# Cross-attention's output step run batch by batch between the units of grouped attention

## What is computed

```
x = x + fp8_product(layernorm(x), ctx)                    # 1
x = x + ternary_ffn(layernorm(x))                         # 2
x = x + cross_attention(layernorm(x), ctx)                # 3: 16 heads of 16, int8 rounding of input and of output
n = layernorm(x);  h = n / rms(n) * ln_w                  # 4: 32 query heads, 8 key heads of 64
n = n + grouped_causal_attention(rope(h @ wq), rope(h @ wk), h @ wv) @ wo
x = x + n + top4_of_16_experts(n / rms(n) * ff_ln_w)
```

## Time and profile before

| | |
|---|---|
| three runs | 795.86, 798.83, 798.04 us; median 798.04 |
| the profiled execution | 799.3 us, its span 797.5 us (1.8 us lie around the span) |
| busy in the span | PE 602.7 us, DVE 557.8, POOL 461.7, ACT 432.0 |
| chain that ended last | PE 50%, DVE 26%, POOL 8%, issue 6%, ACT 6%, DMA 2% |
| cross-attention | about 163 to 285 us |
| the middle | 285 to 319 us |
| prologue | 319 to 341 us |
| the loop | 341 to 613 us |
| router, experts, output | 613 to 797 us |

### The profile page before, as it was taken

The page is one execution under the profiler, slowest core; times in us unless marked ns, Lnnn a source line. Parts: engine busy times, 40 slices in busy tenths (PEclk is TensorE's granted clock), DMA queues, the critical chain, the costliest instruction groups (busy, mean ns, idle before and its releaser), DMA issues.

```text
span 797.5 us, 16092 instructions
## 1 busy us (share of the span) xinstructions
PE 602.7 (76%) x5533; PEld 430.8 (54%) x5533; DVE 557.8 (70%) x1420; ACT 432.0 (54%) x1213; POOL 461.7 (58%) x424
## 2 busy tenths in 40 slices
PE   0226989168888834789999999999885269999960
PEld 0113666156566623457777776777764236666640
DVE  5999558877978877866677577577555755555545
ACT  4823533168768821366666665766652227766640
POOL 1051554258977932278798698677533246777750
PEclk9998897679999977999999999999999559999995
DMA  9500130127545530033032522312501812333427
GB/s 300 187 1 1 37 122 2 57 75 229 161 134 191 159 120 1 0 67 67 15 93 55 92 43 41 68 27 55 185 2 57 356 49 90 108 105 110 104 84 261
DMA packets 83465, 77.97 MB, mean 98 GB/s; under 512 B 49408, under 2 KB 75776, under 8 KB 82880
## 3 DMA queue, kind: packets, MB, share of 16 engines
q1 hardware_dynamic: 78880, 64.33, 27.7%
q0 software_dynamic: 4512, 12.71, 5.5%
HBM read 47.46 MB, written 18.55 MB: 83 GB/s over the span
## 4 chain that ended last, share of the span: by engine, by line
PE 50%; DVE 26%; POOL 8%; issue 6%; ACT 6%; DMA 2%; SPq 1%; POOLq 0%; ACTq 0%; DVEq 0%
PE ps L1787 9%; PE ps L2076 8%; PE ps L2002 5%; PE ps L1986 5%; PE ps L1969 5%; PE ps L2099 4%; PE ps L1844 2%; ACT arena L973 2%; PE ps L1714 2%; DVE arena L1493 2%; POOL arena L831 2%; DVE tiny L1486 2%; PE ps L1732 1%; ACT arena L1058 1%; PE ps L2051 1%
## 5 line engine op out<-in xcount | busy, mean ns | idle before, releaser
L1058 ACT ACTIVATE arena<-ps,tiny 128x128 f32<-128x128 f32 (+1 forms) x256 | 103.9, 418 | 53.8 <-DVE tiny L1486 53.8
L831 POOL TENSOR_TENSOR arena<-arena,tiny 128x512 f32<-128x512 f32 x64 | 93.9, 1467 | 62.9 <-DVE tiny L1497 62.7
L1493 DVE COPY arena<-ps 128x512 f32<-128x512 f32 x64 | 44.3, 692 | 75.3 <-PE ps L1969 75.3
L2076 PE MATMUL ps<-arena 128*128 (+1 forms) x282 | 70.6, 387 | 1.2 <-issue 0.7
L1787 PE MATMUL ps<-arena,xt_hi 128*128 128x512 f16 (+1 forms) x224 | 63.1, 367 | 3.6 <-DVE xt_lo L1275 3.0
L866 POOL DMA_INDIRECT arena<-h_store,arena x47 | 46.0, 979 | 33.3 <-DVE arena L1616 19.3
L1986 PE MATMUL ps<-arena 128*64 128x128 f32 x768 | 56.1, 280 | 11.3 <-DVE arena L1501 11.3
L1486 DVE TENSOR_REDUCE tiny<-ps 128x4 f32<-128x512 f32 x64 | 60.9, 952 | 1.2 <-PE ps L1954 0.9
L1630 DVE SCALAR_TENSOR_TENSOR ps<-ps,arena 128x256 f32<-128x256 f32 x47 | 20.3, 433 | 56.3 <-ACT arena L1110 56.3
L1986 PEld LDWEIGHTS ps<-arena 128*64 128x64 f32 x768 | 41.4, 136 | 32.3 <-issue 23.2
L1952 PE MATMUL ps<-arena 128*128 128x128 f16 (+1 forms) x256 | 58.5, 247 | 0.2 <-ACT arena L1037 0.2
(11 more groups left out here) (293 smaller groups left out, 1724.7 us busy)
## 6 DMA issues: line engine op xcount, KB each, us to landing
e_store<-arena SPq DMA_DIRECT2D x13, 768.0 KB, 4.2
arena<-e_store SPq DMA_DIRECT2D x13, 768.0 KB, 8.6
work<-w_dram SPq DMA_DIRECT2D x27, 256.0 KB, 4.6
xn<-w_dram SPq DMA_DIRECT2D x21, 256.0 KB, 4.7
arena<-w_gate_up_t_dram SPq DMA_DIRECT2D x2, 1024.0 KB, 9.0
arena<-wq_dram SPq DMA_DIRECT2D x2, 1024.0 KB, 7.5
arena<-wo_dram SPq DMA_DIRECT2D x2, 1024.0 KB, 5.2
work<-y_store SPq DMA_DIRECT2D x8, 256.0 KB, 5.2
```

The costliest lines, as they stand in the source:

```text
L831: nc.gpsimd.tensor_tensor(p, p, arec[:, u % 4, :].unsqueeze(2).broadcast_to([P, GH, L]), ALU.mult)\
L1058: nc.scalar.activation(ap_[u % 3][:, h, 0:L], head_scores(u, h), ACT.Exp, bias=anm[:, u % 4, h:h + 1], accum_out=asum[:, u % 4, h:h + 1]). ...
L1493: nc.vector.tensor_copy(apt[:, u % 2, 0, :], ps[:, 3, :]).then_inc(a_pt, 1)
L2076: last = mm(ps[:, 2 + i % 2, :], xg[:, i % 2, x_half * KB + k, :], weights(hidden_weights(slot, w_half, k), i), start=(n == 0), stop=(n == 5))
```

## The change

The end of step 3, from the rounding to the second turn, is now a set of steps for one batch (two tiles). Batch 0 takes them during the last batches of cross-attention and straight after it; batches 1 to 3 take them between the units of the loop, one batch ahead: the batch `nb` that follows the batch of the pass. In each batch of passes, counted 0 to 15: DVE rounds at 14 and 15 of the batch before (batch 1: just ahead of the loop), PE turns at 2, PE multiplies by `wo` at 6, DVE adds and takes statistics at 6, POOL makes the roots at 7, DVE makes `xn` and `work` at 8, PE turns at 9. The sides are placed anew: query group 2 of each batch moves into its own batch, six sides of batch 0 instead of eight run ahead of the loop, and the next batch's keys and values come at 10 to 15. The raw expert buffers change places, `work2` first and `xn` second, the expert after the 13 stored ones goes into `work2`, and the wait for the stored cuts moves from DVE to ACT's first pass.

```
-    own = [(3, 0), (3, 1), (4, 0), (4, 1)]
-    following = [(KEY, 0), (KEY, 1), (VAL, 0), (VAL, 1), (1, 0), (1, 1), (2, 0), (2, 1)]
-    at = [0, 1, 2, 4, 5, 6, 8, 9, 10, 12, 13, 14]
+    own = {0: (2, 0), 1: (2, 1), 4: (3, 0), 5: (3, 1), 7: (4, 0), 8: (4, 1)}
+    following = {10: (KEY, 0), 11: (1, 0), 12: (KEY, 1), 13: (1, 1), 14: (VAL, 0), 15: (VAL, 1)}
...
+TURN_O, OUT_O, TURN_H = 2, 6, 9
...
+            later += [(n, h, u + 2) for h in range(2 if c == KEY else 1)]
...
-        e_raw = [t[:, 0:EW // D, :].rearrange("p t d -> p (t d)") for t in (xn, work2)]
+        e_raw = [t[:, 0:EW // D, :].rearrange("p t d -> p (t d)") for t in (work2, xn)]
...
+        def mid_bank(b, first):
+            return 7 if b else first
```

POOL:

```
+            def root_mid(b):
+                ts = batch_tiles(b)
+                pool.wait_ge(stats_ready, 3 + b + 1)
+                link(nc.gpsimd.tensor_scalar(shifted[:, ts], meanvar[:, ts, 1], LN_EPS, 0.0, ALU.add, ALU.add))
+                link(nc.gpsimd.tensor_tensor(rstd[:, ts], shifted[:, ts], half_neg[:, ts], ALU.pow))
+                link(nc.gpsimd.tensor_tensor(shifted[:, ts], rstd[:, ts], rstd[:, ts], ALU.mult))
+                link(nc.gpsimd.tensor_tensor(shifted[:, ts], shifted[:, ts], meanvar[:, ts, 1], ALU.mult))
+                link(nc.gpsimd.tensor_scalar(shifted[:, ts], shifted[:, ts], LN_EPS, 0.0, ALU.add, ALU.add))
+                nc.gpsimd.tensor_tensor(rstd2[:, ts], shifted[:, ts], half_neg[:, ts], ALU.pow).then_inc(rstd_ready, 1)
...
+                    if n == STORED - 1:
+                        root_mid(0)
                     cut_lo(n)
-            root_layernorm(3)
...
+                if i % AU == OUT_O + 1 and i // AU + 1 < B:
+                    root_mid(i // AU + 1)
```

ACT (`turned_o_hi` and `turned_h_hi` write `xt_hi` of one batch after its turn):

```
+                if i % AU == TURN_O + 1 and i // AU + 1 < B:
+                    turned_o_hi(i // AU + 1)
+                if i % AU == TURN_H + 1 and i // AU + 1 < B:
+                    turned_h_hi(i // AU + 1)
+                if i == 0:
+                    for k in range(2):
+                        act.wait_ge(e_kept[k], 16 * len(range(k, STORED, 2)))
```

DVE (`turned_o_lo` and `turned_h_lo` write `xt_lo`; `o_scale` is the row maximum, one scaling and one reciprocal):

```
+            def o_quantise(b):
+                tiles = range(b * TB, (b + 1) * TB)
+                for t in tiles:
+                    last = nc.vector.tensor_scalar(work[:, t, :], work[:, t, :], recip[:, t:t + 1], 127.0, ALU.mult, ALU.min)
+                link(last)
...
+            def add_cross(b):
+                vec.wait_ge(xo_out, (b + 1) * TB)
+                for t in range(TB):
+                    row = b * TB + t
+                    nc.vector.scalar_tensor_tensor(x[:, row, :], ps[:, mid_bank(b, 1), t * D:(t + 1) * D], 1.0 / WS,
+                                                   x[:, row, :], ALU.mult, ALU.add).then_inc(xo_added, 1)
...
+            def normal_rows(b):
+                vec.wait_ge(rstd_ready, 3 + b + 1)
+                tiles = range(b * TB, (b + 1) * TB)
+                for t in tiles:
+                    last = nc.vector.tensor_scalar(xn[:, t, :], x[:, t, :], meanvar[:, t, 0:1], rstd[:, t:t + 1],
+                                                   ALU.subtract, ALU.mult)
+                link(last)
+                for t in tiles:
+                    last = nc.vector.tensor_scalar(work[:, t, :], xn[:, t, :], rstd2[:, t:t + 1], None, ALU.mult)
+                last.then_inc(src_ready, 1)
...
+                    if more and b == B - 2 and i == XU:
+                        vec.wait_ge(x_normed, TB + 1)
+                        o_scale(0)
+                        o_quantise(0)
...
+                    if not more and i == XU:
+                        turned_o_lo(0)
...
+                else:
+                    add_cross(0)
...
+            vec.wait_ge(e_cut_ready, STORED - 1)
+            normal_rows(0)
+            turned_h_lo(0)
...
+            o_scale(1)
+            o_quantise(1)
             for i in range(UNITS + 3):
...
+                if i % AU == TURN_O + 1 and i // AU + 1 < B:
+                    turned_o_lo(i // AU + 1)
+                if i % AU == TURN_H + 1 and i // AU + 1 < B:
+                    turned_h_lo(i // AU + 1)
                 for n in sides_at(i):
                     if n in ROPES:
                         rope(n)
+                if i // AU + 1 < B:
+                    if i % AU == OUT_O:
+                        add_cross(i // AU + 1)
+                    elif i % AU == TURN_H - 1:
+                        normal_rows(i // AU + 1)
+                if i // AU + 2 < B:
+                    if i % AU == AU - 2:
+                        o_scale(i // AU + 2)
+                    elif i % AU == AU - 1:
+                        o_quantise(i // AU + 2)
```

PE (`turn_mid` turns four blocks of 128 by 128; `project_o` is the product by `wo`, twelve matmuls of 256 columns):

```
+                    if not more and i == XU:
+                        pe.wait_ge(x_masked, B * XU)
+                        turn_mid(0, 0, 0)
+                    if not more and i == XU + 2:
+                        project_o(0)
...
             def project(n):
...
+                if u >= 0:
+                    side_bank_free(u)
+                    if u % AU > TURN_H and b:
+                        pe.wait_ge(xt_ready, 8 + 2 * b + 2)
...
                 for n in sides_at(i):
                     project(n)
+                if i // AU + 1 < B:
+                    nb, at = i // AU + 1, i % AU
+                    if at in (TURN_O, OUT_O, TURN_H):
+                        side_bank_free(i)
+                    if at == TURN_O:
+                        turn_mid(nb, 0, 7)
+                    elif at == OUT_O:
+                        project_o(nb)
+                    elif at == TURN_H:
+                        turn_mid(nb, 1, 7)
                 if 2 <= i < UNITS + 2:
                     a_values(i - 2)
```

More of the change, by code:

```diff
@@ L98, in turns_in_order @@
              (2, 0, -1, 4, "act"), (3, 0, -1, 3, "vec")]
-    at = {(3, 0): 2, (3, 1): 3, (4, 0): 5, (4, 1): 7, (1, 0): 13, (1, 1): 14, (2, 0): 15, (2, 1): 17}
-    keys = {(0, 0): 8, (0, 1): 9, (1, 0): 10, (1, 1): 11}
     later = []
[L102 to L109, removed]
+    for n, (b, c, t, u) in enumerate(SIDE):
+        if n >= 4 and c != VAL:
+            later += [(n, h, u + 2) for h in range(2 if c == KEY else 1)]
     return order + [(n, h, u, None, "dma") for n, h, u in later]
@@ L1397, in cross_attend, with turned_h_lo @@
+            def turned_h_lo(b):
+                vec.wait_ge(xt_hi_ready, 8 + 2 * b + 2)
+                for k in range(KB):
+                    last = nc.vector.scalar_tensor_tensor(xt_lo[:, k, batch_tokens(b)],
+                                                          ps[:, mid_bank(b, 3), k * S:(k + 1) * S], ln_w[:, k:k + 1],
+                                                          xt_hi[:, k, batch_tokens(b)], ALU.mult, ALU.subtract)
+                last.then_inc(xt_ready, 1)
             def cross_attend(b, more):
@@ L1883, in cross_attend, with turn_mid, project_o @@
                     last.then_inc(x_turned_back, 1)
+            def turn_mid(b, step, bank):
+                pe.wait_ge(src_ready, 2 + 2 * b + step + 1)
+                for k in range(KB):
+                    for t in range(TB):
+                        at = k * S + t * P
+                        last = nc.tensor.transpose(ps[:, bank, at:at + P], work[:, b * TB + t, k * P:(k + 1) * P],
+                                                   ident[:, :])
+                last.then_inc(blocks_transposed, 1)
+            def project_o(b):
+                pe.wait_ge(xt_ready, 8 + 2 * b + 1)
+                for t in range(TB):
+                    rows = slice((b * TB + t) * P, (b * TB + t + 1) * P)
+                    products(ps[:, mid_bank(b, 1), t * D:(t + 1) * D],
+                             [((xt_hi[:, k, rows], xt_lo[:, k, rows]), (xwo_hi[:, k, :], xwo_lo[:, k, :]))
+                              for k in range(KB)]).then_inc(xo_out, 1)
             project_q(0)
```

146 lines of the change are left out of this document (82 added, 64 removed).

## The result

The changed kernel takes 805.89 us (median of 4 runs, 804.64 to 809.06), the kernel before 797.87 beside it: ratio 1.0106, 95% interval 1.0081 to 1.013. It is slower by 1.1%; the forecast was 794. Its profiled execution has a span of 803.8 us against 797.5.

A forecast was written before the change was run, and what follows sets the result against it. Middle and prologue were taken as bound by chained waits, the loop by its chain from ring maximum to copy, and by PE with two sides. 799.3 - 24.5 + 20 = 794.8, less 1.3: 793.5, rounded up to 794; range 783 to 807.

The forecast's parts named there:

- Steps 1 and 2: Middle: batch 0's rounding on DVE shows 0.9 us; its turn, split and product end cross-attention 1.3 later, at 287.1.
- Step 3: Middle: POOL's roots for batch 0 start about 285.7, take 4.8 us and end at 290.6.
- Step 4: Middle: batch 0's rows take 1.5 us, turn and split 3.0; first side at 295.1 instead of 319.26.
- Step 5: Prologue, first side to first maximum: 21.1 us, with two ropes fewer, batch 1's rounding and 1.3 for a slow first side.
- two ropes fewer, 4.4: Prologue: leaving out two ropes ahead of the loop saves 4.4 us.
- Slots: Loop: PE's added turns and product in the unit pairs cost 0.9 us a batch (0 to 2.2).
- Key side at 10: Loop pass 10: PE is blocked waiting for DVE's split `turned_h_lo`, 1.65 us a batch (0.8 to 2.4).
- Roots at 7, rows at 8: Loop pair 8-9: POOL's roots delay normalising, DVE's rows wait for POOL; 3.0 us a batch (0.5 to 6).
- slower rival: Loop passes 8 and 15: DVE's row steps queue behind POOL, 5 us a batch more, so 809; chance 18%.
- The rival that gaps take the most of it: Loop: idle gaps absorb most added work, leaving 2.6 us a batch; 781 to 788 us; chance 25%.
- Late keys: Loop: next batch's keys turned too late, its first units wait 4 us, three times: 806; chance 7%.
- Wrong if batches cost over 77 us: Loop: the forecast's sign of being wrong, batches of passes under 70 us or over 77.

The follow-up runs named there:

- late cut: Changed kernel with POOL's last stored cut step (low halves of expert 12) behind DVE's four row steps of batch 0: 800.21 us, ratio 1.0057.
- sides-alone kernel: Kernel before with only the new order of sides and ropes, nothing of the middle moved: 808.26 us, ratio 1.0143.
- sides alone with fitted cut steps: Kernel before with the new order of sides and cut steps at passes 3, 4, 20, 32, 35, 36, 48, 51, 52: 804.69 us, ratio 1.0102.
- combined kernel: Changed kernel with fitted cut steps, key side behind the values, batch 1's rounding early and the last stored cut step late: 790.08 us, ratio 0.9906.
- doubled roots: Changed kernel with POOL's six linked root steps made twice at passes 7, 23 and 39: 810.18 us, ratio 1.0162.
- side 8 moved: Kernel with all four edits, but query sides at 0, 1, 3, 4, 5, 7 and cut steps at other passes: 800.89 us, ratio 1.0026.

## Why the prediction was wrong

**The gain, 20.2 instead of 24.5.** Steps 1 and 2 and the start of the roots held (285.75 against 285.7). Step 3 was 2.1 too dear: the roots of two columns took 2.7 us, `pow` 0.71 each. Step 4 was 3.6 too cheap: from roots to first side 8.1 instead of 4.5, because the rows stood beside `cut_lo(12)`, whose store I had looked at but not what it does to DVE beside it; the late cut shows it. Step 5 was 2.9 too cheap, 24.0 instead of 21.1: "two ropes fewer, 4.4" failed (1.1 in the sides-alone kernel; behind the fourth rope the chain runs over ACT's copies), while the rounding, 3.5 us, showed in full.

**The loop, 27.6 instead of 20: the step that failed is "Slots", 0.9 per batch.** I priced it by PE's pairs, 3.6 in all with batch 3. The sides alone measure 14.4: about half for slots (1.9 in batch 2, 2.1 in batch 3, where cut steps make no difference) and half for cut steps that keep their passes while POOL's rope sums move into them. I went through the change by its new operations; the steps that stay at fixed passes were not among them. The earlier trace rows show POOL without a gap around a side; whether POOL has one behind pass 12 or 24 in the new order was never asked. The sum of the step is also off by itself: four pairs of 8.12 in 67.31 leave 8.7 for the others and not 8.6, and six of these with 8.3 and 7.9 make 68.4, so 1.1 by its own rule; that is small beside the rest.

**Key side at 10.** Issuing it later gave 5.7 back, against 5.0 forecast for the whole step. The wait was 2.4, 1.7 and 2.2, at the upper end, and one clock drop of 1.6 came with it. This is not all of its price: in the combined kernel, without that wait, the three passages are still 4.4 longer in all than in the sides alone with fitted cut steps. In the loop of before PE never stands more than 1.0 us for another engine.

**Roots at 7, rows at 8, the rest.** 27.6 - 14.4 - 5.7 leaves 7.5 for all else, where I had 11.4. Pair 8-9 came to 10.5, 13.5 and 10.8, near the 10.9 and the 12.8 behind a long cut step; that it fits is partly luck. The roots ahead of the rope sum were to make the normalising 2.5 late; at 2.7 us instead of 4.8 it came just in time, and only doubled roots show that chain. What fills the pair is DVE's rows, which wait for whole POOL instructions (the two `xn` steps take 1.49, 4.27 and 2.46 us instead of 0.73; all four rows are 1.4, 4.4 and 1.7 longer than alone). That was the slower rival's mechanism. Its place and sign were right for pass 8; it does not carry the result, since without those rows the kernel is still 0.6% slower than before, and the rounding at 14 and 15, which it charged too, cost nothing. The rival that gaps take the most of it falls: batches cost 6.3 to 11.6 more. Late keys did not show. "Wrong if batches cost over 77 us" came true in batch 1.

The Trainium skill, GPSIMD Engine Reference, Specifications, names contention for VectorE instructions in a two-port mode or with two SBUF inputs. The row steps have one wide SBUF input, and no run shows in which mode they ran; this case shows them waiting for POOL to the end of its instruction, 4.31 us against 0.73.

Open: what sets the price of the slots. With fitted cut steps passages 8 and 9 together are 1.05 longer than before, 12 and 13 as well, and 16 and 17 1.3, while 10 and 11 are 1.3 shorter; no run changed the count of sides. Open too is how much of each passage is the lower clock: it followed PE's long waits, and no run holds the clock apart from the wait.

## What to carry to other kernels

When a change moves work in a static schedule, list what stays at fixed places as well: here steps at every fourth pass fitted the old order and collided with the new one. Price a moved step by what its neighbours on the other engines do in that pass, above all SBUF-to-SBUF steps of DVE beside long POOL instructions. A wait that blocks PE's queue is cheap to mend by issuing it behind work that is ready, 4.8 us here.

## What was not expected of the hardware

- `pow` on POOL goes partly by columns: 0.71 us for two, 1.77 for eight (L809 of before).
- In the full loop the granted clock fell behind single waits of PE. Behind waits of 3.80 us (changed kernel, 437.64) and 3.36 us (side 8 moved, 407.74) it was 0.50, which is 1.2 GHz. Behind a wait of 2.2 to 2.4 us it fell in some executions of the same loop code and not in others: passage 43 took 6.42 in the changed kernel and 8.00 with the late cut, both behind a wait of 2.24 us.
- DVE's last step of a rope ahead of the loop (L1567, two operands in SBUF) took 0.69 us alone and 1.57 us where it started just behind POOL's L832 of 1.16 us.
